# Gates of rows 2 to 7 spread by DMA, their third unit rounded by POOL, and the token sums moved ahead on DVE

## The reference

```python
h = tok(x)                                    # embedding, decaying memory (a scan), LayerNorm, 4 GELU MLP layers, head
h = h + attn(layernorm(h))                    # linear attention, 4 heads
h = h + ffn(layernorm(h))                     # mixture of experts: the stage of this change

def ffn(x):                                   # x: 8 x 512 tokens of 64 channels
    xn = layernorm(x) * gamma + beta
    logits = xn @ Wr + br                     # 8 experts
    top_vals, top_idx = top_k(logits, 2)
    w_full = one_hot(top_idx) @ softmax(top_vals)   # the gate of each token and expert; 6 of 8 are zero
    y = 0
    for e in range(8):
        h = gelu(xn @ W1[e] + b1[e])          # 128 hidden channels
        y = y + (h @ W2[e] + b2[e]) * w_full[..., e, None]
    return y
```

## Time and profile before

| | us |
|---|---|
| median of 3 runs | 407.26 (407.03 to 407.29) |
| the profiled execution | 406.67 |
| its span, first to last instruction | 404.7 |
| granted TensorE clock, mean | 0.997 |

### The profile page before, as it was taken

The page is one execution under the profiler, slowest core; times in us unless marked ns, Lnnn a source line. Parts: engine busy times, 40 slices in busy tenths (PEclk is TensorE's granted clock), DMA queues, the critical chain, the costliest instruction groups (busy, mean ns, idle before and its releaser), DMA issues.

```text
span 404.7 us, 6382 instructions
## 1 busy us (share of the span) xinstructions
PE 382.7 (95%) x1980; PEld 310.7 (77%) x1980; DVE 346.8 (86%) x825; ACT 331.8 (82%) x618; POOL 259.6 (64%) x382
## 2 busy tenths in 40 slices
PE   4999799999999999999999999999998999999995
PEld 2787578888888888888888878778776877786774
DVE  3897879888888988988888889999977899899886
ACT  1688989989999998988977855687887998997982
POOL 0686997787778788778777557586322664454451
PEclk9999999999999999999999999999999999999998
DMA  5900022122122121223312000000000000000001
GB/s 188 385 5 0 2 52 38 42 52 50 32 54 52 26 55 43 46 44 52 47 34 52 2 0 2 0 2 2 1 0 2 1 2 13 14 15 13 15 13 26
DMA packets 15849, 14.93 MB, mean 37 GB/s; under 512 B 9797, under 2 KB 10569, under 8 KB 15561
## 3 DMA queue, kind: packets, MB, share of 16 engines
q1 hardware_dynamic: 15816, 14.54, 14.4%
HBM read 13.42 MB, written 1.11 MB: 36 GB/s over the span
## 4 chain that ended last, share of the span: by engine, by line
PE 64%; DVE 16%; ACT 8%; issue 5%; POOL 3%; DMA 2%; SPq 1%; DVEq 0%; ACTq 0%
PE ps L1566 58%; PE ps L1589 4%; ACT w_all L919 2%; DVE hid L1432 1%; ACT x L913 1%; ACT hid L913 1%; DVE hh L1328 1%; DVE kstat L1268 1%; DVE x L1284 1%; DVE x L1432 1%; DMA xn<-in_w_f 1%; DMA rstd_row<-roots 1%; DVE qmax L1280 1%; DVE qsum L1294 1%; PE ps L1770 1%
## 5 line engine op out<-in xcount | busy, mean ns | idle before, releaser
L1113 DVE TENSOR_TENSOR hid_lo<-hid,hid_hi 128x1024 fp32r<-128x1024 f32 x64 | 78.9, 1233 | 25.2 <-ACT hid_hi L751 25.1
L746 ACT ACTIVATE hid<-ps,b_fold 128x512 f32<-128x512 f32 x128 | 83.8, 682 | 18.7 <-PE ps L1566 18.3
L1566 PE MATMUL ps<-xn_hi,w_all 128*128 128x512 f32 x256 | 88.3, 404 | 1.3 <-DVE xn_lo L1108 1.3
L1566 PE MATMUL ps<-hid_hi,w_all 128*128 128x512 f32 x256 | 85.0, 393 | 0.0
L751 ACT ACTIVATE hid_hi<-hid 128x1024 fp32r<-128x1024 f32 x64 | 67.9, 1061 | 2.0
L1566 PEld LDWEIGHTS ps<-xn_hi,w_all 128*128 128x128 f32 x256 | 48.4, 189 | 12.4 <-DVE xn_lo L1108 2.7
L1566 PEld LDWEIGHTS ps<-hid_hi,w_all 128*128 128x128 f32 x256 | 48.0, 188 | 9.9
L1566 PE MATMUL ps<-xn_lo,w_all 128*128 128x512 f32 x128 | 49.9, 390 | 0.0
L1566 PE MATMUL ps<-hid_lo,w_all 128*128 128x512 f32 x128 | 49.8, 389 | 0.0
L1566 PE MATMUL ps<-hid_hi,ew 128*128 128x512 f32 x131 | 41.2, 400 | 0.7 <-ACT memT L855 0.4
L537 POOL TENSOR_TENSOR var_in<-var_in 128x4 f32<-128x4 f32 x32 | 36.5, 1142 | 2.6
(11 more groups left out here) (232 smaller groups left out, 920.0 us busy)
## 6 DMA issues: line engine op xcount, KB each, us to landing
rstd_row<-roots SPq DMA_DIRECT2D x29, 256.0 KB, 3.8
hh<-in_tokens SPq DMA_DIRECT2D x8, 256.0 KB, 7.8
hid<-in_w SPq DMA_DIRECT2D x1, 1024.0 KB, 7.5
rstd_row<-in_w SPq DMA_DIRECT2D x1, 1024.0 KB, 9.8
out<-hh SPq DMA_DIRECT2D x7, 128.0 KB, 2.0
ew_raw<-in_expert_w SPq DMA_DIRECT2D x1, 512.0 KB, 9.1
roots<-rstd SPq DMA_DIRECT2D x29, 2.0 KB, 1.4
ew_raw<-in_expert_w SPq DMA_DIRECT2D x1, 256.0 KB, 9.2
```

Of the source, the lines that this page charges most:

```text
L746: act.activation(hid[:, j % 2, f, :], bank[f], ACT.Gelu, bias=b1_fold[:, j // B * F + f:j // B * F + f + 1]).then_inc(gelu_done, 1)
L1113: dve.tensor_tensor(hid_lo[:, j % 2, 2 * p:2 * p + 2, :], hid[:, j % 2, 2 * p:2 * p + 2, :], hid_hi[:, j % 2, 2 * p:2 * p + 2, :].bitcast( ...
L1566: return pe.matmul(out, lhsT, rhs, start=start, stop=stop)
```

## The change

1. **Gates by DMA.** For rows 2 to 7 (units 16 to 61) PE no longer spreads the gate. `gates_out` also writes half the gates, a token on each partition, to `gates_tok`; SP stores them to DRAM (`gates_rows`, in pieces of 16 bytes) and loads each unit's line to all partitions of one of four slots of `gate_spread` (which is `rstd_row`). The product reads `gate_spread` at a step of four elements, and waits for its load and for its slot of `hw`. The output stores stand between the loads in SP's order.
2. **Third unit.** In rows 2 to 7 the unit of expert 2 is rounded by POOL instead of ACT, and DVE makes its residue one unit later.
3. **Token sums.** `alone_sum(62)` moves ahead of row 6's output, `alone_sum(63)` right behind it; both wait for both products.

```diff
 LO_BY_DVE = (0, 2, 4, 6)
+HI_BY_POOL = 2
 UNITS = B * E
+BY_DMA = 2 * E
 WHOLE = (E + 3, 2 * E + 3)
...
 GROUPS = ((0, 4), (4, 2), (6, 2))
+GROUPS_ROWS = ((0, 1, 2, 3), (4, 5), (6, 7))
 GROUP_OF = (0, 0, 0, 0, 1, 1, 2, 2)
...
     return sum(split(k) for k in range(n))
+def hi_by_pool(n):
+    return split(n) and n % E == HI_BY_POOL and n >= 2 * E
+def rounded_by_act(n):
+    return sum(split(k) and not hi_by_pool(k) for k in range(n))
 def lo_by_dve(n):
     return split(n) and (n % E in LO_BY_DVE or n == UNITS - 3)
+def spread_by_dma(n):
+    return n >= BY_DMA and not alone(n)
+def not_last(n):
+    return sum(not alone(k) and not ends_row(k) for k in range(n + 1))
+def loaded(n):
+    return sum(spread_by_dma(k) for k in range(n % 4, n + 1, 4))
 def ends_row(n):
...
         KEXP = S + NMEM
+        gates_hbm = nc.dram_tensor("gates_rows", (B, E, S), fp32).ap()
+        gates_tok = sb("gates_tok", [P, B, E, NT])
+        gate_spread = rstd_row
         roots_hbm = nc.dram_tensor("roots", (4, P * NT), fp32).ap()
...
         hw_ready, hwhi_act = sem("hw_ready"), sem("hwhi_act")
+        gates_split, gates_stored, multiplied = sem("gates_split"), sem("gates_stored"), sem("multiplied")
+        gates_loaded = [sem("gates_loaded%d" % k) for k in range(4)]
         alone_done, alone_taken = sem("alone_done"), sem("alone_taken")
         hwlo_dve, hwlo_pool = sem("hwlo_dve"), sem("hwlo_pool")
+        hwhi_pool = sem("hwhi_pool")
         e2_done, y_done, y_copied = sem("e2_done"), sem("y_done"), sem("y_copied")
...
                 sp.dma_start(rstd_row[:, slot, :], roots_hbm[slot].partition_broadcast(P)).then_inc(rstd_loaded, 16)
-            for b in range(B):
+            def store_gates(p):
+                sp.wait_ge(gates_split, p + 1)
+                for b in GROUPS_ROWS[p]:
+                    sp.dma_start(gates_hbm[b].rearrange("e (p t) -> p e t", t=NT),
+                                 gates_tok[:, b, :, :]).then_inc(gates_stored, 16)
+            def load_gates(n):
+                b, e = divmod(n, E)
+                if n == BY_DMA:
+                    sp.wait_ge(ctx_done, B)
+                if n >= BY_DMA + 4:
+                    sp.wait_ge(hw_ready, gated(n - 3))
+                sp.wait_ge(gates_stored, 16 * (GROUPS_ROWS[GROUP_OF[b]][-1] + 1))
+                sp.dma_start(gate_spread[:, n % 4, :], gates_hbm[b, e].partition_broadcast(P)).then_inc(gates_loaded[n % 4], 16)
+            def store_output(b):
                 dst = out_hbm[b, :, :].rearrange("(t p) c -> p t c", p=P)
...
                     sp.dma_start(dst[:, t, :], tiles(h1[:, b, :])[:, t, :]).then_inc(stored[(b + k) % 2], 16)
+            store_gates(0)
+            for n in range(BY_DMA, UNITS):
+                m, u = divmod(n, E)
+                if u == 5:
+                    store_output(m - 2)
+                if n == 3 * E + 4:
+                    store_gates(1)
+                if n == 6 * E - 1:
+                    store_gates(2)
+                if spread_by_dma(n):
+                    load_gates(n)
+            store_output(B - 2)
+            store_output(B - 1)
             sp.wait_ge(stored[0], 16 * (B // 2 + 1))
...
                 slot = n % NSLOT
-                pool.wait_ge(hwhi_act, rounded(n + 1))
+                pool.wait_ge(hwhi_act, rounded_by_act(n + 1))
                 pool.tensor_tensor(hw_lo(slot), hw(slot), hw_hi[:, slot * S:(slot + 1) * S].bitcast(fp32),
                                    ALU.subtract).then_inc(hwlo_pool, 1)
+            def hidden_hi(n):
+                slot = n % NSLOT
+                pool.wait_ge(hw_ready, gated(n + 1))
+                pool.tensor_copy(hw_hi[:, slot * S:(slot + 1) * S], hw(slot)).then_inc(hwhi_pool, 1)
             for n in range(UNITS):
...
                     hidden_lo(n)
+                if hi_by_pool(n):
+                    hidden_hi(n)
         @block.scalar
...
                     gelu(n + LEAD)
-                if 1 <= n <= UNITS and split(n - 1):
+                if 1 <= n <= UNITS and split(n - 1) and not hi_by_pool(n - 1):
                     hidden_hi(n - 1)
...
                                   ALU.subtract).then_inc(gates_ready, 1)
+                rows = GROUPS_ROWS[p]
+                dve.tensor_scalar(gates_tok[:, rows[0]:rows[-1] + 1, :, :],
+                                  wgt[:, r, :].rearrange("p (b t) e -> p b e t", t=NT),
+                                  0.5, None, ALU.mult).then_inc(gates_split, 1)
             def dve_job(n):
...
                 dve.wait_ge(eg_done, n + 1)
+                if spread_by_dma(n):
+                    dve.wait_ge(gates_loaded[n % 4], 16 * loaded(n))
+                    if ends_row(n - NSLOT):
+                        dve.wait_ge(y_done, (n - NSLOT) // E + 1)
+                    else:
+                        dve.wait_ge(multiplied, not_last(n - NSLOT))
+                    dve.tensor_tensor(hw(slot).rearrange("p (t q) -> p t q", t=NT),
+                                      hg(n % NHG).rearrange("p (t q) -> p t q", t=NT),
+                                      gate_spread[:, n % 4, :].rearrange("p (q t) -> p t q", t=NT),
+                                      ALU.mult).then_inc(hw_ready, 1)
+                    return
                 dve.wait_ge(wb_done, gated(n + 1))
...
                 slot = n % NSLOT
-                dve.wait_ge(hwhi_act, rounded(n + 1))
+                if hi_by_pool(n):
+                    dve.wait_ge(hwhi_pool, sum(hi_by_pool(k) for k in range(n + 1)))
+                else:
+                    dve.wait_ge(hwhi_act, rounded_by_act(n + 1))
                 dve.tensor_tensor(hw_lo(slot), hw(slot), hw_hi[:, slot * S:(slot + 1) * S].bitcast(fp32),
...
                 k = ALONE.index(n)
-                dve.wait_ge(alone_done, k + 1)
+                dve.wait_ge(alone_done, len(ALONE))
                 own.wait(own.n)
...
                     gates_out(p, v)
-                if u == 0 and n == UNITS + E:
+                if n == UNITS:
                     alone_sum(UNITS - 2)
-                    alone_sum(UNITS - 1)
                 if u == 0 and n >= 2 * E:
                     output(m - 2)
-                if 1 <= n <= UNITS and lo_by_dve(n - 1):
+                if n == UNITS:
+                    alone_sum(UNITS - 1)
+                if 1 <= n <= UNITS and lo_by_dve(n - 1) and not hi_by_pool(n - 1):
                     hidden_lo(n - 1)
+                if 2 <= n < UNITS + 2 and hi_by_pool(n - 2):
+                    hidden_lo(n - 2)
         @block.tensor
...
                 e = n % E
-                if n == 2 * E:
-                    pe.wait_ge(h1_ready, B)
                 last = last_use(n, spread_bank)
-                if last is not None and n != 2 * E:
+                if last is not None:
                     pe.wait_ge(hw_ready, gated(last + 1))
...
                     pe.wait_ge(hw_ready, gated(n + 1))
-                    mm(bank[6 + b % 2], w2_whole[:, WHOLE_EXPERTS.index(e), :], hw(slot), start=False, stop=False)
+                    mm(bank[6 + b % 2], w2_whole[:, WHOLE_EXPERTS.index(e), :], hw(slot),
+                       start=False, stop=False).then_inc(multiplied, 1)
                     return
...
                     last.then_inc(y_done, 1)
+                else:
+                    last.then_inc(multiplied, 1)
             def turn_sum(b):
...
                         pe.wait_ge(h1_ready, 7)
-                    if not alone(n):
+                    if n == 2 * E:
+                        pe.wait_ge(h1_ready, B)
+                    if n < BY_DMA:
                         spread_gates(n)
```

## The result

The changed kernel takes 439.59 us (median of 4 runs, 439.02 to 442.84), beside 407.27 us (4 runs, 407.03 to 408.37) for the kernel before: 1.0815 times as long, 95% interval 1.0788 to 1.0842. The forecast was 427.9 us, range 415 to 438. So the direction and its main reason hold, and the size doesn't: +32.3 us where I said +20.6. The profiled execution has a span of 437.4 us, against 404.7 us before.

A forecast was written before the change was run, and what follows sets the result against it. The bound changes hands in rows 2 to 7; then DVE and POOL exclude each other: 82.6 against 66.5 us (+16.1), with cover and handovers +21.4, end -0.8, so +20.6 on 407.26: 427.9 us, range 415 to 438.

The forecast's parts named there:

- What bounds the kernel: Rows 2 to 7: the bound changes hands among ACT, DVE and PE; DVE busy 59.6 of 66.5 us.
- The exclusion: Rows 2 to 7: DVE operations with two SBUF inputs and POOL's streaming operations run one after the other, 82.6 us.
- my floor of 16.1: Rows 2 to 7: extra us if exclusive DVE work and POOL work run one after the other, 82.6 against 66.5.
- cover that isn't used: Of 7.7 us DVE work that may run beside POOL, 40% won't: 3.1 us, ends 0 and 7.7.
- handovers: Each of 28 POOL operations breaks DVE's overlap of two operations, 0.68 against 0.60 us: 2.2 us.
- The step: Products' gate read at 16 bytes: taken 0.60 us, bounds 0.60 and 1.2; as rival at most 28 us, 440 to 455, 6%.
- The gate stores: SP's queue before loads of units 28 and 47: 3 to 5 us a pair, costing nothing at the slower pace.
- The copy on POOL: Six new 128x512 copies in POOL's queue, 0.7 us each, 4.2 us in all, ends 0.6 and 1.58 each.
- The third unit's relief: Six roundings leave ACT for POOL, 3.8 us less ACT; ACT is covered, so it brings nothing.
- The sums: End of the kernel: both token sums moved ahead leave DVE 4.0 us instead of 4.7 after its last residue: 0.8 less.
- PE's clock: Rival: with PE less busy, clock granted 1.2 GHz, a row's PE work up to 18 us, about 445 us; 3%.
- The rival without exclusion: Products in rows 2 to 7 pass POOL untouched, ACT and PE relief counts: about 404.3 us, faster; 6%.

The follow-up runs named there:

- experiment 2: Changed kernel, but from unit 16 on POOL's residues and roundings are two zeroings each, so POOL only writes; 423.48 us, ratio 1.0400.
- experiment 7: Changed kernel with PE's gate spreading kept for all units and products reading the PSUM bank; loads, stores and waits stay; 417.40 us, ratio 1.0245.
- experiment 1: Changed kernel, but the product reads gate_spread in one run of 512 elements instead of at a step of four; 425.63 us, ratio 1.0458.
- experiment 3: Changed kernel with the gate read in one piece and POOL only zeroing from unit 16 on; 411.14 us, ratio 1.0083.
- experiment 5: Changed kernel with only the gate stores altered, to pieces of 128 bytes; 438.01 us, ratio 1.0775.
- experiment 4: Changed kernel with gate read in one piece, POOL only zeroing, and gate stores in pieces of 128 bytes; 404.25 us, ratio 0.9938.
- experiment 9: Parts run separately: gates by DMA alone 437.29 us; in the kernel before, sums alone 406.00, third unit on POOL alone 408.05, these two together 407.18.

## Why the prediction was right and wrong

**What bounds the kernel: right.** That rows 2 to 7 leave DVE no room was the base of all, and DVE's 32.7 us more became 32.7 us of span, one for one.

**The exclusion: right in kind, its size within the sum.** Products with two SBUF inputs and POOL's subtractions hold each other, as L1104 did in the earlier trace rows; experiments 2 and 7 show it from both sides. Its price has no run of its own. Experiment 2 gives 16.1 us and experiment 1 less experiment 3 gives 14.5, both with old holds freed and a shorter POOL operation in them. Experiment 1 is 8.2 us longer than experiment 7, where POOL does its full work in both; but experiment 7 keeps PE's 46 matmuls and has 3.1 us more of stalls. So the price lies between 8 and 16 us, at or under my floor of 16.1. The 3.1 us for cover that isn't used and the 2.2 for handovers on top of it aren't seen. As a check, experiment 1 is the kernel I reckoned with: 425.6 us, where I forecast 427.9, and it has in it two stalls at the stores, of 2.4 and 3.5 us, that I had left out. So without the step the forecast would have been 2 to 8 us too high, not low. One thing I had wrong in the mechanism: I let a POOL operation wait for one DVE operation, 1.9 us at most with its own work, and single ones took 4.59 us in after and 7.13 in experiment 5.

**The step: the term that failed.** I bounded a product between 0.60 and 1.2 us and took 0.60, "as the contiguous form is the nearest row". The step that failed is the sentence "By themselves they keep their price": a product was 1.07 us by itself against 0.68. No row was near: none showed a step at all, and a bound of twice the price on 46 operations was a term of 28 us, more than my whole forecast. It cost 14.0 us (experiment 1; 12.3 where POOL only writes, experiment 2 less experiment 3). Worse, I made it a rival at 6%, as if it were an alternative to the exclusion, and its 440 to 455 us was the forecast with the step added: the two are independent and both hold. A term with a bound on each side belongs in the sum, at a weighed value. With half of the bound, 14 us, and my other terms as they stood I would have said 442.
The Trainium skill, "SBUF — State Buffer", section Door 1, gave the reason to do so: it wants two accesses or more to each 16-byte line for full bandwidth. The runs agree: at a step of 8 bytes two numbers share a line, and the operation took 0.68 us; at 16 bytes each lies in a line of its own, and it took 1.07. The same note counts four fp32 as free to stride; read as a step of four, that isn't what was measured.

**The gate stores: wrong on the size, right on the cover.** I bounded the pair at 3 to 5 us to landing and said that it costs nothing at the slower pace. One of these stores takes 5.4 us by the median, a pair landed after 6.0, and the loads behind them land after about 7. I had the load of unit 48 wait; it was those of units 28 and 47, which need nothing of these stores and only stand behind them in SP's queue. DVE did stand idle 4.3 us for that, but taking it away gave 1.6 us (experiment 5). At today's pace, where I said it could lose at most 2 us, it is 6.9 us by the medians of experiments 3 and 4, and 5.9 by their ratios. I had taken landing time from the output store's 512 pieces by count, and no row had pieces of 16 bytes.

**The copy on POOL: right.** 0.62 us unheld for the 0.7 I took; held by products it went up to 1.47.

**The third unit's relief: nothing, as said, and a little less than that.** I had counted its exclusion only inside the sum. Alone it costs 1.4 us; experiment 9 shows one hold of it, not the whole.

**The sums: right alone, not seen in the change.** -0.8 forecast, -0.85 measured alone, with an interval of about -0.4 to -1.7. In the changed kernel the stretch behind the last product grew from 8.2 to 9.5 us all the same, with PE's clock lower.

**PE's clock: seen, and a small term that I had at nothing.** It fell to 0.73 in one window of 15 us while DVE was the bound, which cost nothing that a run shows, and to 0.68 behind the last product, where some 2 us went with it. As the rival that makes PE the bound of every row it didn't come.

**The rival without exclusion: its price met by a kernel that is more than it.** I gave 404.3 us for products that pass as they did before, and experiment 4, with contiguous reads and quick stores, took 404.25 us. But POOL reads nothing in it, so it has also lost the waiting that the kernel before has, 2.4 us in L1374 and L1384 by my own sum. The match is in part luck, and how much the relief of PE and ACT is worth stays open. It was never enough for what it cost.

The account of +32.3 us goes best in steps from 439.59 down, each a run: POOL's reads away, 16.1 us (423.48); the step away too, 12.3 (411.14, alone it is 14.0); the stalls at the stores away too, 6.9 (404.25, alone 1.6). That is 35.3 us, and 404.25 is 3.0 under the 407.27 of before (2.4 under the 406.68 beside it). POOL's share has in it the holds that the kernel before has too, and each step some of PE's clock at the end, so these are steps between runs and not pure prices. The third unit's 1.4 us isn't a term of its own in it.

## What to carry to other kernels

Before an operand moves from PSUM to SBUF, look at who streams reads from SBUF at the same time: on a DVE with little idle time, 46 products that each had one SBUF input cost 8 to 16 us more with two. Read the access pattern of a new operand as a price of its own, and where no row shows it, measure it or put half of its bound into the sum: bounds that belong to every one of many instructions aren't rivals. And a small DMA in many tiny pieces is not small for the large one in the queue behind it.

## What the runs showed of the hardware

- A DVE multiplication of 128x512 fp32 with the second input at a step of 8 bytes takes 0.68 us, as in one piece; at 16 bytes it takes 1.06 to 1.13 us.
- POOL zeroing 128x512 (0.52 us) doesn't hold a DVE operation with two SBUF inputs and isn't held by it (33 meetings, 45 of 46 products at 1.06 to 1.12 us); POOL subtracting does: 2.0 to 2.17 us for 12 of the 34 products that met it.
- Eight DVE operations with two SBUF inputs, back to back, held one POOL subtraction for 7.13 us instead of 1.3 (experiment 5).
- Behind the last product the same DVE work took 9.5 us at a granted clock of 0.68 and 7.3 us at 0.87 to 1.00.
- A store of 16 KB as 1024 pieces of 16 bytes lands in 5.0 to 5.6 us by the median, the same as 128 pieces of 128 bytes in 2.0 to 2.4 us; a load of 256 KB behind two of the first kind lands in 6.8 to 8.7 us instead of 3.2 to 3.5.
